# GpSimd issues the gathers of two units in a row, then the scatters of two units, and a scatter waits for the third one ahead of it instead of for the whole unit ahead

## The chip, the cores and the metric

The kernel runs on one core of a Trainium2 chip. A core has five engines that run their own instruction streams: TensorE (PE in the profile, with PEld for its weight loads), VectorE (DVE), ScalarE (ACT), GpSimd (POOL) and SyncE (SP). They meet at semaphores. The metric is the device time of one execution in microseconds; shorter is better.

## The reference

There are 50,000 nodes with 128 features and 50,000 edges, sorted by receiver. Each edge takes its sender's features, projects them, mixes them with its direction and with weights from a small network of its length, and adds the result to its receiver. Each node is then normalised.

```python
xs = s @ W_up0 / f32(MUL) ** 0.5
xv = jnp.einsum('nmc,mk->nkc', v, W_up1) / f32(MUL) ** 0.5
ss = xs[senders]                       # gather
vv = xv[senders]
m0 = w[:, 0] * ss                      # w: the network's weights of the edge
m1 = w[:, 1][:, :, None] * ss[:, :, None] * Y1[:, None, :]
m2 = w[:, 2][:, :, None] * vv
m3 = w[:, 3] * (jnp.einsum('emc,ec->em', vv, Y1) / SQ3)
msg_s = jax.ops.segment_sum(mid_s, receivers, num_segments=num_nodes)   # scatter and add
msg_v = jax.ops.segment_sum(mid_v, receivers, num_segments=num_nodes)
x = _layernorm(x + out, axis=-1)       # out: the projected sums
```

The input draws the receivers as 50,000 times the square of a uniform number and sorts them, so that nodes of low number have many edges and nodes of high number have few.

## The kernel before

The edges are cut into 98 units (UNITS) of four tiles (G); a tile is 128 edges. They are worked off from the high receivers down. For each tile GpSimd issues a gather (`sender<-in_x_dram,index`, L420), an indirect DMA that fetches 128 rows of x by the edges' senders. TensorE transposes and projects the rows, computes the weights and sums edges of one tile that have the same receiver; VectorE makes the products; ScalarE moves results out of PSUM and writes the unit's message (`msg`, L641 and L642) into one of four slots (RING). Then GpSimd issues for each tile a scatter (`acc<-msg,index`, L444), an indirect DMA that adds 128 rows of the message onto the array acc in HBM. acc starts as a copy of x, made in 80 pieces that SyncE issues (L295) while the first units run. Once no later unit can touch a chunk of nodes, SyncE loads it from acc (L331), VectorE takes its moments, ScalarE normalises it, and SyncE stores it (L345); a table (`dense_orders`) says after which pair of units each chunk may be loaded.

Two scatters that add to the same row must not be in flight together. Within a tile this is met by the sums; between tiles by waits. A scatter counts up a semaphore of its own when it lands. In the kernel before, the first scatter of a unit waits for all four of the unit ahead (L435). The others wait for the one just ahead of them only if the table `scatter_orders` flags that two tiles of the unit have overlapping ranges of receivers (`meets`), except in units 0 and 1, where they always wait (L442). So that neighbouring tiles do not stand in one unit, `turns` (L272) deals the eight tiles of two rows of edges out to an even and an odd unit.

The order on GpSimd is written out by hand (L448 to L456): the gathers of six units (LAG), then for each unit v the four gathers of unit v + 6 and the four scatters of unit v. A gather waits, at the first tile of a unit, for all gathers of two units ahead (L416) and for TensorE to have used the slot of eight units ahead (L418). The message slots tie ScalarE to GpSimd: the message of unit v waits until the scatters of unit v - 4 have landed (L640).

## Time and profile before

| | us |
|---|---|
| median of three runs | 1323.9 (1321.33 to 1324.72) |
| the profiled execution | 1335.3 |
| its span, first to last instruction | 1333.5 |
| granted TensorE clock, mean | 0.831 |
| GpSimd busy | 1014.3 (76% of the span) |
| TensorE busy | 928.8 (70%) |
| VectorE busy | 692.2 (52%) |
| ScalarE busy | 537.5 (40%) |

An indirect DMA is issued by GpSimd; its busy time in the profile is the time in which it makes the descriptors, and the data land afterwards. Between two such instructions the profile shows about 0.30 us in which the engine is idle and waits for nothing that the profile shows ("issue"). "remote" is a wait whose releaser the profile cannot name.

### The profile page before, as it was taken

The numbers are of one execution on the slowest core, as the hardware profiler recorded it, in microseconds if no ns is written. First come the engines' busy times: TensorE is split into PE (matmuls) and PEld (weight loads), VectorE is DVE, ScalarE is ACT, GpSimd is POOL, SyncE is SP. The second block draws the span as 40 slices with busy tenths as digits, with TensorE's granted clock in tenths as the row PEclk, the third lists the DMA queues.
The fourth block names the chain that finished last, engine by engine and source line by source line (L and its number), as shares of the span: only waits on it lengthen the run. The fifth ranks groups of instructions, "written<-read, shape, count | busy, mean of one in ns | idle before, by whom it ended". The sixth has DMA issues, their size and how long they took to land.

```text
span 1333.5 us, 25760 instructions
## 1 busy us (share of the span) xinstructions
PE 928.8 (70%) x6206; PEld 871.6 (65%) x6206; DVE 692.2 (52%) x2882; ACT 537.5 (40%) x1403; POOL 1014.3 (76%) x817
## 2 busy tenths in 40 slices
PE   2577688787788867776876768777876766767800
PEld 1477577787677766766776767676776766767700
DVE  5364334465576456556556466465465556555402
ACT  5233233244445534444444444434443434534301
POOL 6347878888888888888888888888888888888761
PEclk7588877887888889889879897788788888898955
DMA  4377786433443443453453453443444444443332
GB/s 131 113 184 161 168 185 120 94 65 67 114 97 67 93 116 69 90 119 69 90 120 67 91 118 69 93 110 73 94 92 91 94 92 93 93 91 68 59 28 63
DMA packets 82548, 130.36 MB, mean 98 GB/s; under 512 B 16168, under 2 KB 66763, under 8 KB 81232
## 3 DMA queue, kind: packets, MB, share of 16 engines
q0 software_dynamic: 68992, 51.43, 28.7%
q1 hardware_dynamic: 12888, 77.27, 17.3%
q10 hardware_dynamic: 632, 1.29, 0.3%
q14 instruction: 27, 0.22, 0.1%
q8 instruction: 9, 0.15, 0.0%
HBM read 78.31 MB, written 77.22 MB: 117 GB/s over the span
## 4 chain that ended last, share of the span: by engine, by line
issue 31%; POOL 28%; DMA 11%; PE 8%; another core or an unknown queue 7%; SPq 5%; ACT 4%; POOLq 3%; ACTq 1%; DVE 0%; DVEq 0%
POOL acc L444 20%; POOL sender L420 7%; DMA acc<-msg,index 6%; DMA acc<-in_x_dram 5%; SPq L295 3%; PE ps_msg L553 2%; PE ps_sum L541 2%; ACT normed L693 2%; PE ps_wts L528 2%; POOLq L427 1%; PE ps_hid L512 1%; PE ps_dst L494 1%; PE ps_sT L500 1%; ACT hid L656 1%
## 5 line engine op out<-in xcount | busy, mean ns | idle before, releaser
L444 POOL DMA_INDIRECT acc<-msg,index x392 | 621.1, 1585 | 170.3 <-issue 111.0
L420 POOL DMA_INDIRECT sender<-in_x_dram,index x392 | 386.8, 987 | 123.5 <-issue 111.9
L541 PE MATMUL ps_sum<-same,mid 128*128 128x128 f32 x1568 | 248.0, 310 | 1.5 <-issue 0.8
L541 PEld LDWEIGHTS ps_sum<-same,mid 128*128 128x128 f32 x1568 | 240.3, 226 | 10.0 <-DVE mid L930 0.8
L915 DVE TENSOR_TENSOR wts<-ps_wts,bias 128x512 f32<-128x512 f32 x98 | 67.8, 692 | 323.2 <-PE ps_wts L528 205.4
L528 PE MATMUL ps_wts<-mlp,hid 128*128 128x128 f32 x784 | 139.4, 335 | 104.9 <-ACT hid L668 100.6
L632 ACT COPY sumT<-ps_sum 128x512 f32<-128x512 f32 x196 | 114.9, 587 | 235.5 <-remote 131.3
L553 PE MATMUL ps_msg<-outw,sumT 128*128 128x64 f32 x1568 | 202.0, 285 | 2.3 <-ACT sumT L632 1.6
L553 PEld LDWEIGHTS ps_msg<-outw,sumT 128*128 128x128 f32 x1568 | 200.0, 206 | 3.2 <-issue 1.2
L528 PEld LDWEIGHTS ps_wts<-mlp,hid 128*128 128x128 f32 x784 | 126.6, 245 | 111.8 <-ACT hid L668 107.0
L512 PE MATMUL ps_hid<-hid,mlp 128*128 128x256 f32 x196 | 78.8, 490 | 150.2 <-ACT hid L656 110.1
L693 ACT ACTIVATE normed<-total,shift,rstd 128x128 f32 x391 | 157.0, 484 | 56.4 <-DVE shift L981 50.4
L908 DVE TENSOR_TENSOR proj<-ps_up,vec_all 128x384 f32<-128x384 f32 x98 | 54.4, 555 | 208.0 <-remote 137.9
L521 PE MATMUL ps_up<-up,senderT 128*128 128x128 f32 x784 | 131.9, 319 | 28.8 <-issue 10.4
L512 PEld LDWEIGHTS ps_hid<-hid,mlp 128*128 128x128 f32 x196 | 35.8, 228 | 162.6 <-ACT hid L656 118.6
L641 ACT COPY msg<-ps_msg 128x128 f32 (+1 forms) x98 | 26.1, 266 | 283.6 <-DMA acc<-msg,index 134.8
L521 PEld LDWEIGHTS ps_up<-up,senderT 128*128 128x128 f32 x784 | 111.2, 219 | 43.1 <-issue 21.8
L944 DVE BATCH_NORM_STATS2 stats<-total 128x6 f32 x391 | 79.5, 278 | 56.8 <-DMA total<-acc 56.2
L881 DVE CUSTOM_DVE_ANT_0 junk<-same,earlier 128x128 f32<-128x128 f32 x392 | 91.4, 289 | 3.4
L507 PE MATMUL ps_hid<-basisT,mlp 32*128 32x128 f32 x392 | 75.4, 315 | 13.8 <-ACT basisT L648 9.8
L650 ACT COPY senderT<-ps_sT 128x512 f32<-128x512 f32 x98 | 56.8, 579 | 62.3 <-remote 32.3
L500 PE MATMUL ps_sT<-ident,sender 128*128 128x128 f32 x392 | 71.5, 314 | 8.9 <-DMA sender<-in_x_dram,index 8.9
(135 smaller groups left out, 1061.5 us busy)
## 6 DMA issues: line engine op xcount, KB each, us to landing
acc<-in_x_dram SPq DMA_DIRECT2D x80, 312.5 KB
total<-acc SPq DMA_DIRECT2D x30, 832.0 KB
out_dram<-normed SPq DMA_DIRECT2D x29, 832.0 KB
sender<-in_x_dram,index POOLq DMA_INDIRECT x392
acc<-msg,index POOLq DMA_INDIRECT x392
out_dram<-normed ACTq DMA_DIRECT2D x1, 832.0 KB
vec_raw<-in_edge_attr_dram SPq DMA_DIRECT2D x1, 576.0 KB
acc<-zeros SPq DMA_DIRECT2D x1, 320.0 KB, 3.9
```

The costliest lines, as they stand in the source:

```text
L420: pool.indirect_dma_start(sender[:, u % SRING, i, :], None, x, bass.IndirectOffsetOnAxis(ap=index[:, u, 0, i:i + 1], axis=0)).then_inc(gat ...
L444: pool.indirect_dma_start(acc, bass.IndirectOffsetOnAxis(ap=index[:, v, 1, i:i + 1], axis=0), msg[:, v % RING, i, :], None, compute_op=ALU.add
L500: mm = pe.transpose(ps_sT[:, P * i:P * (i + 1)], sender[:, k % SRING, i, :], ident[:, :])
L512: pe.matmul(ps_hid[:, 2:4, :], mlp1[:, :], hid0[:, k % 2, :], start=True, stop=True).then_inc(hid1_ps, 1)
L521: mm = pe.matmul(ps_up[:, i, :], senderT[:, b, P * i:P * (i + 1)], up[:, :], start=True, stop=True)
L528: mm = pe.matmul(ps_wts[:, i, :], hid1[:, b, P * (i // 2):P * (i // 2 + 1)], mlp2[:, i % 2, :], start=True, stop=True)
L541: mm = pe.matmul(ps_sum[r][:, i, h, :], mid[:, b, 2 * r + i, P * h:P * (h + 1)], same[:, b, 2 * r + i, :], start=True, stop=True)
L553: mm = pe.matmul(ps_msg[:, i, 2 * MUL * h:2 * MUL * (h + 1)], sumT[:, b, i, h, :], outw[:, h, :], start=True, stop=True)
L632: act.copy(sumT[:, b, 2 * r:2 * r + 2, :, :], ps_sum[r][:, :, :, :]).then_inc(sum_ready[r], 1)
L693: mm = act.activation(normed[0:parts, b, r, :], total[0:parts, quarter, r, :].rearrange("p b d -> p (b d)"), ACT.Identity, scale=rstd[0:pa ...
L881: mm = dve.tensor_tensor_reduce(junk[:, b, i, :], same[:, b, i, :], earlier[:, :], 1.0, 0.0, ALU.mult, ALU.add, count[:, b, i:i + 1])
L944: mm = dve.bn_stats(stats[0:parts, r, :], total[0:parts, quarter, r, :].rearrange("p b d -> p (b d)"))
```

## The change

LAG stays at six, and BATCH = 2 is new. After the first six units' gathers, GpSimd issues the gathers of units v + 6 and v + 7 in a row, eight of them, and then the eight scatters of units v and v + 1.

Count all scatters through, n = 4v + i. Scatter n now waits for scatter n - 3 to have landed, always. It waits for n - 1 (and, at the first tile of a unit, for n - 2) only if the unit's flag is set; without the flag that wait asks for a count that an older landing has already brought. The flag is now made from the ranges of tiles one and two places apart in this count, over unit borders too. `turns` deals the tiles in another order within the unit, so that those at distance one and two are not neighbours. The extra waits for units 0 and 1 are gone.

Each gather now has its own semaphore by tile (`gathered`, and `slot_done` for the first two units), and gather i of unit u waits for gather i of unit u - 1, four issues ahead. `slot_done` is the new name of `scattered` and starts with the 16 counts of a gather, so all that is compared with it is 16 higher. TensorE waits for the four gathers of its unit one by one. The table of flags takes other instructions on VectorE, and one more memset on GpSimd.

```diff
 LAG = 6
+BATCH = 2
...
-        meet = sb("meet", [1, UNITS, G * (G - 1) // 2])
-        meet_too = sb("meet_too", [1, UNITS, G * (G - 1) // 2])
+        meet = sb("meet", [1, 2, TILES])
+        meet_too = sb("meet_too", [1, 2, TILES])
...
-            return a.rearrange("p (j w) (q r) -> p w q j r", w=2, r=2)[:, w]
+            return a.rearrange("p (j w) (r q) -> p w q j r", w=2, r=2)[:, w]
...
-                    sp.wait_ge(scattered[1][i], 16 * j + 16)
+                    sp.wait_ge(slot_done[1][i], 16 * j + 32)
...
+            pool.memset(meet[:, :, :], 0.0)
...
+            def landed(n):
+
+                return slot_done[n // G % 2][n % G], 16 * (n // G // 2) + 32
+
+            def here(u, i):
+
+                return (slot_done[u][i], 16) if u < 2 else (gathered[u % 2][i], 16 * (u // 2))
+
             def gathers(u):
 
-                if u >= 2:
-                    pool.wait_ge(gathered[u % 2], 16 * G * (u // 2))
                 if u >= SRING:
                     pool.wait_ge(senderT_ps, u - SRING + 1)
                 for i in range(G):
+                    if u >= 1:
+                        pool.wait_ge(*here(u - 1, i))
                     pool.indirect_dma_start(sender[:, u % SRING, i, :], None, x,
                                             bass.IndirectOffsetOnAxis(ap=index[:, u, 0, i:i + 1], axis=0)
-                                            ).then_inc(gathered[u % 2], 16)
+                                            ).then_inc(here(u, i)[0], 16)
...
-                if v >= 1:
-                    for i in range(G):
-                        pool.wait_ge(scattered[1 - c][i], 16 * ((v + 1) // 2))
                 for i in range(G):
-                    if i >= 1:
-
-                        if v >= 2:
-                            pool.wait_ge(scattered[c][i - 1], 16 * (v // 2) + 16 * meets)
-                        else:
-                            pool.wait_ge(scattered[c][i - 1], 16)
+                    n = G * v + i
+                    if n >= 3:
+                        pool.wait_ge(*landed(n - 3))
+                    for of in (n - 2, n - 1) if i == 0 else (n - 1,):
+                        if of >= 0:
+
+                            to, count_after = landed(of)
+                            pool.wait_ge(to, count_after - 16 + 16 * meets)
...
-            for v in range(UNITS):
-                if v + LAG < UNITS:
-                    gathers(v + LAG)
-                scatters(v)
+            for v in range(0, UNITS, BATCH):
+                for u in range(v + LAG, min(v + LAG + BATCH, UNITS)):
+                    gathers(u)
+                for u in range(v, v + BATCH):
+                    scatters(u)
...
-                pe.wait_ge(gathered[b], u * (16 * G // 2) + 16 * G - 16 * G * b // 2)
...
+                    if k < 2:
+                        pe.wait_ge(slot_done[b][i], 16)
+                    else:
+                        pe.wait_ge(gathered[b][i], 8 * (u - b))
                     mm = pe.transpose(ps_sT[:, P * i:P * (i + 1)], sender[:, k % SRING, i, :], ident[:, :])
...
-                        act.wait_ge(scattered[b][i], 8 * (v - b) - 8 * RING + 16)
+                        act.wait_ge(slot_done[b][i], 8 * (v - b) - 8 * RING + 32)
...
-                at = 0
-                for apart in range(1, G):
-                    n = G - apart
-                    dve.tensor_tensor(meet[:, :, at:at + n], high[:, :, 0:n], low[:, :, apart:G], ALU.is_ge)
-                    mm = dve.tensor_tensor(meet_too[:, :, at:at + n], high[:, :, apart:G], low[:, :, 0:n], ALU.is_ge)
-                    at += n
+                lo, hi = (a[:, :, :].rearrange("p v i -> p (v i)") for a in (low, high))
+                for apart in range(1, 3):
+                    n = TILES - apart
+                    dve.tensor_tensor(meet[:, apart - 1, apart:TILES], hi[:, 0:n], lo[:, apart:TILES], ALU.is_ge)
+                    mm = dve.tensor_tensor(meet_too[:, apart - 1, apart:TILES], hi[:, apart:TILES], lo[:, 0:n], ALU.is_ge)
                 link(mm)
...
```

**Order on GpSimd at the start.** The engine's stream from the last gathers before the first scatter on, before; `sender` is the gathers' target, `acc<-msg` a scatter, and the names in brackets are the semaphores that a row waits for.

```order
L420 DMA sender<-in_x_dram,index 128x128 [waits gathered0,scatter_tables,spare_rows]
L420 DMA sender<-in_x_dram,index 128x128 x3
L427 TENSOR_LOAD scatter_orders
L427 ISA x2
L428 ISA
L429 ISA [waits acc_init0]
L444 DMA acc<-msg,index 50640x128 [waits msg_ready,acc_init1,rows_ready]
L444 DMA acc<-msg,index 50640x128 [waits scattered0_0]
L444 DMA acc<-msg,index 50640x128 [waits scattered0_1]
L444 DMA acc<-msg,index 50640x128 [waits scattered0_2]
```

And now:

```order
L431 DMA sender<-in_x_dram,index 128x128 [waits gathered0_0]
L431 DMA sender<-in_x_dram,index 128x128 [waits gathered0_1]
L431 DMA sender<-in_x_dram,index 128x128 [waits gathered0_2]
L431 DMA sender<-in_x_dram,index 128x128 [waits gathered0_3]
L437 TENSOR_LOAD scatter_orders
L437 ISA x2
L438 ISA
L439 ISA [waits acc_init0]
L453 DMA acc<-msg,index 50640x128 [waits msg_ready,acc_init1,rows_ready]
L451 ISA
L453 DMA acc<-msg,index 50640x128 [waits slot_done0_0]
L453 DMA acc<-msg,index 50640x128 [waits slot_done0_1]
```

Before, the gathers of unit 6 are the last ahead of the first scatter, and each further scatter of unit 0 waits for the one ahead. Now the gathers of unit 7 stand ahead of the first scatter too, and the waits for the scatter just ahead ask only for a count that the gather of the slot brought; the fourth scatter waits for the first.

**Order on GpSimd in the middle.** The stream from unit 8's gathers to unit 9's, before:

```order
L420 DMA sender<-in_x_dram,index 128x128 [waits senderT_ps,gathered0]
L420 DMA sender<-in_x_dram,index 128x128 x3
L427 TENSOR_LOAD scatter_orders
L427 ISA x2
L428 ISA
L429 ISA [waits acc_init0]
L444 DMA acc<-msg,index 50640x128 [waits scattered1_1,scattered1_2,scattered1_0,scattered1_3,msg_ready,acc_init1,rows_ready]
L440 ISA
L444 DMA acc<-msg,index 50640x128 [waits scattered0_0]
L444 DMA acc<-msg,index 50640x128 [waits scattered0_1]
L444 DMA acc<-msg,index 50640x128 [waits scattered0_2]
L420 DMA sender<-in_x_dram,index 128x128 [waits senderT_ps,gathered1]
```

And now, from unit 3's scatters to the gathers that follow:

```order
L439 ISA [waits acc_init0]
L451 ISA [waits msg_ready,slot_done0_1,rows_ready,acc_init1]
L453 DMA acc<-msg,index 50640x128 [waits slot_done0_2,slot_done0_3]
L453 DMA acc<-msg,index 50640x128 [waits slot_done0_2,slot_done1_0]
L453 DMA acc<-msg,index 50640x128 [waits slot_done0_3,slot_done1_1]
L453 DMA acc<-msg,index 50640x128 [waits slot_done1_0,slot_done1_2]
L431 DMA sender<-in_x_dram,index 128x128 [waits gathered1_0,senderT_ps]
L431 DMA sender<-in_x_dram,index 128x128 [waits gathered1_1]
L431 DMA sender<-in_x_dram,index 128x128 [waits gathered1_2]
L431 DMA sender<-in_x_dram,index 128x128 [waits gathered1_3]
L431 DMA sender<-in_x_dram,index 128x128 [waits gathered0_0,senderT_ps]
L431 DMA sender<-in_x_dram,index 128x128 [waits gathered0_1]
```

Before, four gathers and four scatters take turns, and the first scatter waits for four landings at once. Now eight of a kind stand in a row; each scatter names two semaphores, one of the third scatter ahead, and each gather names one.

**Order on GpSimd at the end.** The last two units, where no gathers are left, before:

```order
L440 ISA
L444 DMA acc<-msg,index 50640x128 [waits scattered0_0]
L444 DMA acc<-msg,index 50640x128 [waits scattered0_1]
L444 DMA acc<-msg,index 50640x128 [waits scattered0_2]
L427 TENSOR_LOAD scatter_orders
L427 ISA x2
L428 ISA
L429 ISA [waits acc_init0]
L444 DMA acc<-msg,index 50640x128 [waits scattered0_1,scattered0_2,scattered0_0,scattered0_3,msg_ready,acc_init1,rows_ready]
L440 ISA
```

And now:

```order
L453 DMA acc<-msg,index 50640x128 [waits slot_done1_2,slot_done1_3]
L451 REGISTER_ALU [waits slot_done1_2]
L453 DMA acc<-msg,index 50640x128 [waits slot_done0_0]
L453 DMA acc<-msg,index 50640x128 [waits slot_done1_3,slot_done0_1]
L453 DMA acc<-msg,index 50640x128 [waits slot_done0_0,slot_done0_2]
L437 TENSOR_LOAD scatter_orders
L437 ISA x2
L438 ISA
L439 ISA [waits acc_init0]
L451 ISA [waits msg_ready,slot_done0_1,rows_ready,acc_init1]
L453 DMA acc<-msg,index 50640x128 [waits slot_done0_2,slot_done0_3]
L453 DMA acc<-msg,index 50640x128 [waits slot_done0_2,slot_done1_0]
```

The wait for the whole unit ahead has gone from the unit's first scatter; what stands there now names tiles 1, 2 and 3 of the unit ahead, of which only tile 1 must have landed when the flag is not set.

## Rows read from the trace of the kernel before

**Rows 1.** Page, busy us, share of the span and instructions.
```profile
PE 928.8 (70%) x6206; PEld 871.6 (65%) x6206; DVE 692.2 (52%) x2882; ACT 537.5 (40%) x1403; POOL 1014.3 (76%) x817
```

**Rows 2.** Groups of POOL by line: busy, mean ns; idle before, releasers.
```profile
L444 POOL DMA_INDIRECT acc<-msg,index x392 | 621.1, 1585 | 170.3 <-issue 111.0 <-DMA acc<-msg,index 37.9 <-ACT msg L642 20.5
L420 POOL DMA_INDIRECT sender<-in_x_dram,index x392 | 386.8, 987 | 123.5 <-issue 111.9 <-DMA acc<-msg,index 6.4 <-DVE index L753 4.3
```

**Rows 3.** Waits of POOL's scatters for landings: us in total, times, longest.
```profile
POOL acc L444 <- DMA acc<-msg,index: 37.9, 24, 3.8
```

**Rows 4.** Timeline of POOL, start: start us, us, what, idle before.
```profile
46.88 0.95 POOL L420 DMA_INDIRECT sender<-in_x_dram,index  x1 [0.30 <-issue]
68.34 1.64 POOL L444 DMA_INDIRECT acc<-msg,index  x1 [20.51 <-ACT msg L642]
73.10 1.57 POOL L444 DMA_INDIRECT acc<-msg,index  x1 [3.13 <-DMA acc<-msg,index]
```

**Rows 5.** Timeline of POOL, middle: gathers of a unit, scatters of a unit.
```profile
704.83 1.02 POOL L420 DMA_INDIRECT sender<-in_x_dram,index  x1 [0.30 <-issue]
706.15 0.98 POOL L420 DMA_INDIRECT sender<-in_x_dram,index  x1 [0.30 <-issue]
707.44 0.95 POOL L420 DMA_INDIRECT sender<-in_x_dram,index  x1 [0.30 <-DMA acc<-msg,index]
...
709.94 1.62 POOL L444 DMA_INDIRECT acc<-msg,index  x1 [0.30 <-issue]
711.87 1.58 POOL L444 DMA_INDIRECT acc<-msg,index  x1 [0.30 <-issue]
...
715.62 1.60 POOL L444 DMA_INDIRECT acc<-msg,index  x1 [0.30 <-issue]
```

**Rows 6.** Timeline of POOL, the end: unit 91's last scatter, unit 92's first, the last.
```profile
1249.24 1.57 POOL L444 DMA_INDIRECT acc<-msg,index  x1 [0.30 <-issue]
1253.37 1.55 POOL L444 DMA_INDIRECT acc<-msg,index  x1 [2.56 <-DMA acc<-msg,index]
...
1307.45 1.57 POOL L444 DMA_INDIRECT acc<-msg,index  x1 [0.30 <-issue]
```

**Rows 7.** Timeline of SP after the last scatter.
```profile
1312.17 0.35 SPq L331 DMA_DIRECT2D total<-acc  x1
```

**Rows 8.** Timeline of ACT: the messages of units 0, 1, 2 and 9.
```profile
66.69 0.69 ACT L642 COPY msg<-ps_msg 128x384 f32<-128x384 f32 x1
...
74.24 0.67 ACT L642 COPY msg<-ps_msg 128x384 f32<-128x384 f32 x1
...
92.11 0.69 ACT L642 COPY msg<-ps_msg 128x384 f32<-128x384 f32 x1
...
182.18 0.69 ACT L642 COPY msg<-ps_msg 128x384 f32 x1
```

**Rows 9.** Timeline of POOL: the first scatter of unit 9.
```profile
199.87 1.62 POOL L444 DMA_INDIRECT acc<-msg,index  x1 [0.30 <-issue]
```

**Rows 10.** Timeline of PE and DVE during the first gathers.
```profile
34.50 2.07 PE L521 MATMUL ps_up<-up,senderT 128*128 128x128 f32 x8
...
52.26 0.56 DVE L908 TENSOR_TENSOR proj<-ps_up,vec_all 128x384 f32<-128x384 f32 x1 [17.40 <-remote]
```

**Rows 11.** Timeline of ACT: the messages of units 52 and 53.
```profile
707.71 0.67 ACT L642 COPY msg<-ps_msg 128x384 f32 x1
719.33 0.68 ACT L642 COPY msg<-ps_msg 128x384 f32 x1
```

**Rows 12.** Timeline of POOL: the last scatter of unit 48.
```profile
702.92 1.60 POOL L444 DMA_INDIRECT acc<-msg,index  x1 [0.30 <-issue]
```

**Rows 13.** Page, DMA issues: the transfers of the chunks.
```profile
total<-acc SPq DMA_DIRECT2D x30, 832.0 KB
out_dram<-normed SPq DMA_DIRECT2D x29, 832.0 KB
```

**Rows 14.** Timeline of DVE: the first instruction after the flags' table.
```profile
28.75 0.36 DVE L785 TENSOR_SCALAR norm<-norm 128x392 f32<-128x392 f32 x1 [3.37 <-ACT norm L609]
```

More of the change, by code:

```diff
@@ L61 @@
 RSQRT_BITS = float(0x5f3759df)
-assert UNITS % 2 == 0 and LAG <= SRING and (UNITS - 2) % SRING == 0 and UNITS <= P and FULL == UNITS - 1 and FULL >= 96
+assert UNITS % 2 == 0 and LAG <= SRING and UNITS % BATCH == 0 and LAG % BATCH == 0 and (UNITS - 2) % SRING == 0 and UNITS <= P and FULL == UNITS - 1 and FULL >= 96
 assert NORM_AFTER > STATS_AFTER and NORM_AFTER > RING // 2 and (UNITS - 2) % RING == 0 and CHUNKS % 2 == 0 and PIECES % 2 == 0 and N % PIECE == 0 and REST <= P
@@ L208, in bass_gnn @@
         sp_passed = sem("sp_passed")
-        gathered = [sem(f"gathered{b}") for b in range(2)]
+        gathered = [[sem(f"gathered{b}_{i}") for i in range(G)] for b in range(2)]
         basis_staged = sem("basis_staged")
@@ L234, in bass_gnn @@
         msg_ready = sem("msg_ready")
-        scattered = [[sem(f"scattered{b}_{i}") for i in range(G)] for b in range(2)]
+        slot_done = [[sem(f"slot_done{b}_{i}") for i in range(G)] for b in range(2)]
         total_in = [sem(f"total_in{b}") for b in range(2)]
@@ L419, in gathers @@
                 for i in range(G):
+                    if u >= 1:
+                        pool.wait_ge(*here(u - 1, i))
                     pool.indirect_dma_start(sender[:, u % SRING, i, :], None, x,
                                             bass.IndirectOffsetOnAxis(ap=index[:, u, 0, i:i + 1], axis=0)
-                                            ).then_inc(gathered[u % 2], 16)
+                                            ).then_inc(here(u, i)[0], 16)
             def scatters(v):
-                c = v % 2
                 order = pool.value_load(scatter_orders[0:1, v:v + 1], min_val=2, max_val=2 * PIECES - 1)
@@ L445, in scatters @@
                                             msg[:, v % RING, i, :], None, compute_op=ALU.add
-                                            ).then_inc(scattered[c][i], 16)
+                                            ).then_inc(slot_done[v % 2][i], 16)
             pool.wait_ge(index_in, 1)
@@ L801, in make_scatter_orders @@
             def make_scatter_orders():
-                at = 0
-                for apart in range(1, G):
-                    n = G - apart
-                    dve.tensor_tensor(meet[:, :, at:at + n], high[:, :, 0:n], low[:, :, apart:G], ALU.is_ge)
-                    mm = dve.tensor_tensor(meet_too[:, :, at:at + n], high[:, :, apart:G], low[:, :, 0:n], ALU.is_ge)
-                    at += n
-                link(mm)
-                link(dve.tensor_tensor(meet[:, :, :], meet[:, :, :], meet_too[:, :, :], ALU.mult))
-                link(dve.tensor_reduce(meet_unit[:, :], meet[:, :, :], AX_X, ALU.max))
+                lo, hi = (a[:, :, :].rearrange("p v i -> p (v i)") for a in (low, high))
[3 more added lines that the diff above has]
+                    mm = dve.tensor_tensor(meet_too[:, apart - 1, apart:TILES], hi[:, apart:TILES], lo[:, 0:n], ALU.is_ge)
+                link(mm)
+                for apart in range(1, 3):
+                    mm = dve.tensor_tensor(meet[:, apart - 1, apart:TILES], meet[:, apart - 1, apart:TILES],
+                                           meet_too[:, apart - 1, apart:TILES], ALU.mult)
+                link(mm)
+                link(dve.tensor_tensor(meet[:, 0, :], meet[:, 0, :], meet[:, 1, :], ALU.max))
+                link(dve.tensor_reduce(meet_unit[:, :], meet[:, 0, :].rearrange("p (v i) -> p v i", i=G), AX_X, ALU.max))
                 link(dve.tensor_reduce(pieces[:, :], high[:, :, :], AX_X, ALU.max))
```

## The prediction

> **What bounds the kernel now.** I read the shares of the engines first. None is near 100%: GpSimd is busy for 76% of the span, TensorE for 70% [rows 1]. The groups by line say what that hides. GpSimd issues 784 indirect DMAs, busy 621.1 + 386.8 = 1007.9 us, and ahead of each stands the 0.30 us that the profile calls issue, 784 x 0.30 = 235 us [rows 2]. Together that is 1243 us of a span of 1333.5 us. The timeline of the middle shows the same: gathers and scatters follow each other at 0.30 us, and GpSimd waits for nobody [rows 5]. So GpSimd's issue is the path, and a change is worth what it takes out of GpSimd's stream or out of its waits. What is left of the span are the first 11.6 us, a wait of 20.51 us for the first message [rows 4], waits for landings, and the end after the last scatter (1307.45 + 1.57 to 1333.5, 24.5 us), which loads, normalises and stores the last chunk [rows 6, 7].
>
> The waits view gives the third of these. Scatters wait for landings 24 times, 37.9 us in all, 3.8 us at the longest [rows 3]. Less the 0.30 us of issue that each has anyway, 24 x 0.30 = 7.2 us, 30.7 us are true waits. The timeline says where: three within unit 0 and three within unit 1, the first of them 3.13 us [rows 4], and one ahead of each of units 92 to 97, where no gathers are left to issue in the meantime. The first of those six is 2.56 us, 2.26 us over issue [rows 6]; six of them make 13.6 us, and 17.1 us remain for units 0 and 1. The other twelve of the 24 end within the issue time. In units 2 to 91 a unit's first scatter comes 5 us of gathers after the last scatter of the unit ahead, and the wait is over by then.
>
> **The change part by part.** The sum is made against the profiled execution (span 1333.5 us, 1335.3 us with what lies around it) and taken off the median, 1323.9 us. The profiled one is 11.4 us longer; I don't know where, and that matters below.
>
> *The end.* Units 92 to 97 no longer wait for the last scatter, but for the third one ahead. From the end of its issue to the due time of the scatter in question lie two further scatters and three times issue, about 2 x 1.57 + 3 x 0.30 = 4.04 us [rows 6]. The wait for the nearest landing lasted 2.56 us, so the new wait is over in time. Saved: 13.6 us. What is late next here is nothing of TensorE's: the message slots are full (below), and a unit of scatters takes 7.5 us.
>
> *The start.* Units 0 and 1 lose their six waits (17.1 us). Also, the gathers of unit 7 now come ahead of the first scatter, into the 20.51 us in which GpSimd waits for message 0: four gathers at 0.95 + 0.30 and 0.10 for the switch (next but one), 5.1 us that are not on the path any more. That would be 22.2 us. But GpSimd would then run into the messages. They are ready at 67.38, 74.91 and 92.80 us for units 0 to 2, and at 182.87 us for unit 9 [rows 8], whose scatter starts at 199.87 us [rows 9]: 17.0 us of slack, the least that I found among units 3 to 17. From message 0 to its scatter it took 68.34 - 67.38 = 0.96 us [rows 4, 8]. So not more than 17.0 - 0.96 = 16.0 us can be had unless the messages come faster, and I take 16.0 us. Units 0 to 3 themselves fit: scatters of units 0 and 1 to 68.34 + 8 x 1.87 = 83.3 us, eight gathers to 93.4 us, and message 2 is there at 92.8 us. One bound is the full 22.2 us. The other: VectorE started on unit 0 at 52.26 us, though TensorE had its input ready at 36.57 us, and what released it the profile can't name [rows 10]; that is 4.4 us after the last gather's end at 47.83 us [rows 4]. If the early gathers are what holds the other engines back, the four more of unit 7 move every message by 5.1 us, and 10.9 us are left.
>
> *Fewer switches.* The first two gathers after scatters take 1.02 and 0.98 us against 0.95, the first two scatters after gathers 1.62 and 1.58 us [rows 5] against 1.55 and 1.57 where none came between [rows 6]. A pair of units has one switch each way less: 0.10 us from the gathers, up to 0.08 us from the scatters if none of it is the load of the table, which stays. 46 pairs with gathers: 4.6 to 8.3 us. I take 6.
>
> *New waits, scatters.* Scatters 3 to 7 of a run of eight wait for one that was issued in the same run, with the same 4.04 us of room. The landings that the rows show are seen 2.56 us after the end of the issue at the end of the program and at most 3.8 us in units 0 and 1, beside the copies of x. In the middle, ScalarE writes a message as soon as the scatters of four units ahead have landed: unit 53's starts 1.95 us after the issue's end (719.33 - 0.16 for the copy ahead of it, less 715.62 + 1.60), unit 52's 3.03 us (707.55 less 702.92 + 1.60) [rows 5, 11, 12]. All within the room, so the lower end is nothing lost. The upper end: 59 chunks are loaded or stored meanwhile [rows 13]. If each pushed one landing past the longest seen by half of its spread over the shortest, (3.8 - 2.56) / 2 = 0.62 us, 3.8 + 0.62 - 4.04 = 0.38 us would be lost 59 times, 22 us. The nearest rows, those of the middle, are at the lower end; I take 8 us, for gathers and scatters together.
>
> *New waits, gathers.* Each waits for the fourth one ahead; the room is three gathers at 1.25 and 0.30, 4.05 us, as wide as for scatters. Behind a gather that waits stand the rest of the run and then the scatters, so a loss here is as dear. It is in the 8 us.
>
> *More semaphores per instruction.* The first scatter of a unit, with seven semaphores and a table load, has the same 0.30 us ahead of it as the others and is 0.07 us longer [rows 5]. 0.01 us for each of 780 instructions with one more wait would be 7.8 us; I take nothing, since the sequencer does it while the instruction ahead runs.
>
> *Others.* The flags' table is rebuilt on VectorE with longer rows; VectorE then idles 3.37 us for ScalarE [rows 14], which hides the half microsecond. The other order of tiles within a unit costs nothing. TensorE's clock plays no part: message 52 is written between the scatters of units 48 and 49 [rows 5, 11, 12], over three units early, and that slack of some 40 us hides that the message slots now come free in pairs.
>
> Sum: 16.0 + 13.6 + 6 - 8 = 27.6 us, 1323.9 - 27.6 = 1296 us.
>
> **The rivals.** (a) The messages don't limit the start. Half of the 11.4 us by which the profiled execution is longer may be just the unnamed waits of the other engines; without them messages come sooner and the start gives 22.2 us. With the losses as above 34 us are saved (1290 us), with none and the full 8.3 us of switches 44 us (1280 us). Against it: the slack of 17.0 us is a row.
>
> (b) The early gathers hold back the messages: 10.9 at the start, 22.5 us in all, 1301 us; with the upper 22 us for lost room 8.5 us, 1315 us. For it speaks the 4.4 us between the last gather and VectorE's start.
>
> (c) Slower than before: with eight scatters in a row the landing of each takes longer, because three of them are in flight with no gathers between. In a run of eight, scatter 3 waits for 0 and scatter 6 for 3, so a landing seen x us beyond the room costs 2x in each of 49 pairs. The gain without losses is 35.6 us; it is gone at 35.6 / 98 = 0.36 us, that is from landings at 4.40 us on. At 3.8 + 1.24 (the whole spread once more) = 5.04 us the cost is 98 x 1.00 = 98 us, and the kernel takes 1323.9 + 62 = 1386 us. Against it: scatters in a row at the end land in 2.56 us.
>
> The rows show a landing 1.95 to 3.8 us after the issue. The Trainium skill, "DMA: Bandwidth & Descriptors", section "Latency and other measured facts", says that HBM answers in 0.2 us on average and in 2 us at high load, and that this is most of a DMA's fixed cost. By that rule a loaded stretch would add 1.8 us to the 2.56 us, 4.36 us, 0.32 us over the room, 31 us in 98 waits, and leave 4 us of gain (1320 us). The spread from 1.95 to 3.8 us agrees that load matters; that it reaches this far everywhere no row shows.
>
> (d) The change doesn't do what it says: the flag is set for most units, so each scatter waits for the one ahead as in unit 0. That is 2.26 us for each of some 380 scatters, 860 us. In the kernel before no unit but 0 and 1 waits within the unit, so no two tiles at that distance overlap, and the new order keeps tiles at distance one and two equally far apart.
>
> **How the numbers follow.** Forecast 0.50; (a) 0.24; (b) 0.19; (c), the case of the skill's rule included, 0.06; (d) 0.01. The forecast's own range is 1290 to 1302 us. Taking in most of (a) and of (b), I reach from 1282 to 1311 us. A measurement can tell 0.3% from no change, 4 us. All of the forecast, (a) and nearly all of (b) are faster than that: 0.92. No change needs (b) with more losses than its upper end, or the skill's rule: 0.04. Slower is the rest of (c) and (d): 0.04.
>
> **What would show it.** In the profile after: the gathers of unit 7 ahead of the first scatter; no wait within unit 0, and a wait for messages in the first 200 us; after the last gather 24 scatters and more in a row at 1.87 us, without a gap of 2.56 us; pairs of units at about 25.2 us instead of 25.4; POOL's waits for landings below 10 us in all, each well under 1 us. Wrong would be: waits for landings at scatters 3 and 6 of most runs, waits for messages after the first 250 us, or a first message later than 70 us.

## The result, and the profile after

The changed kernel takes 1285.41 us (median of four runs, 1283.88 to 1289.08); the kernel before took 1323.8 us beside it (four runs, 1321.33 to 1324.72). The ratio is 0.9717, with a 95% interval of 0.9692 to 0.9742: 37.5 us faster by the ratio, where 27.6 us were forecast. The time lies in the predicted range of 1282 to 1311 us, 10.6 us under the predicted value.

The profiled execution of the changed kernel took 1289.08 us, with a span of 1287.3 us. From its page, the engines' busy time (us, share of the span, instructions) and POOL's two groups by line (busy, mean ns; idle time ahead, releaser), to be read against [rows 1, 2]:

```profile
PE 862.5 (67%) x6206; PEld 819.2 (64%) x6206; DVE 693.7 (54%) x2882; ACT 535.3 (42%) x1403; POOL 1005.5 (78%) x818
...
L453 POOL DMA_INDIRECT acc<-msg,index x392 | 617.3, 1575 | 128.6 <-issue 110.2
L431 POOL DMA_INDIRECT sender<-in_x_dram,index x392 | 381.0, 972 | 127.8 <-issue 110.4
```

GpSimd is busy for 8.8 us less. The greater part went from its idle time: 170.3 to 128.6 us ahead of the scatters, while the gathers gave back 4.3 us. The wait for a message, 20.5 us in the row of before, has gone from the list.

The waits of POOL (us in total, times, longest), against [rows 3]:

```profile
POOL acc L453 <- issue: 110.2, 344, 1.3
POOL acc L453 <- DMA acc<-msg,index: 14.2, 40, 1.0
POOL sender L431 <- DMA sender<-in_x_dram,index: 12.2, 25, 2.5
```

Each of them contains the 0.30 us of issue. Over all 784 instructions, what goes beyond issue (0.31 us at the most) comes to 9.0 us ahead of the scatters and 4.9 us ahead of the gathers, if GpSimd's wait for its first indices is left out; part of it stands under "issue" (1.3 us at the longest), where the profile names no releaser. Some 11 of these 13.9 us fall ahead of unit 20, where copies of x still run beside.

The start on POOL's timeline (start us, us, what, idle before), against [rows 4]:

```profile
52.87 1.03 POOL L431 DMA_INDIRECT sender<-in_x_dram,index  x1 [0.30 <-DMA acc<-in_x_dram]
54.21 1.63 POOL L453 DMA_INDIRECT acc<-msg,index  x1 [0.30 <-DMA acc<-in_x_dram]
56.15 1.57 POOL L453 DMA_INDIRECT acc<-msg,index  x1 [0.30 <-issue]
58.02 1.55 POOL L453 DMA_INDIRECT acc<-msg,index  x1 [0.30 <-issue]
...
62.56 1.55 POOL L453 DMA_INDIRECT acc<-msg,index  x1 [0.94 <-DMA acc<-in_x_dram]
...
80.51 1.62 POOL L453 DMA_INDIRECT acc<-msg,index  x1 [0.30 <-issue]
...
86.86 1.56 POOL L453 DMA_INDIRECT acc<-msg,index  x1 [0.91 <-DMA acc<-msg,index]
...
157.57 0.94 POOL L431 DMA_INDIRECT sender<-in_x_dram,index  x1 [2.49 <-DMA sender<-in_x_dram,index]
```

The first scatter follows the last gather of unit 7 at once, 14.1 us earlier than in [rows 4], and the next two come at issue distance. The message is not what it waits for: ACT's timeline has messages 0, 1 and 2 far ahead of their place in [rows 8].

```profile
52.42 0.69 ACT L655 COPY msg<-ps_msg 128x384 f32<-128x384 f32 x1
...
59.97 0.67 ACT L655 COPY msg<-ps_msg 128x384 f32<-128x384 f32 x1
...
75.61 0.69 ACT L655 COPY msg<-ps_msg 128x384 f32<-128x384 f32 x1
```

Message 0 is ready at 53.11 us against 67.38 us, and message 1 at 60.64 us, ahead of unit 1's first scatter at 62.56 us. Nothing in the change makes messages come 14 us sooner. This was the first thing to settle.

The middle, a run of eight scatters and the gathers after it, against [rows 5]:

```profile
695.99 1.62 POOL L453 DMA_INDIRECT acc<-msg,index  x1 [0.30 <-issue]
697.92 1.59 POOL L453 DMA_INDIRECT acc<-msg,index  x1 [0.30 <-issue]
...
711.00 1.02 POOL L431 DMA_INDIRECT sender<-in_x_dram,index  x1 [0.30 <-issue]
712.33 0.98 POOL L431 DMA_INDIRECT sender<-in_x_dram,index  x1 [0.30 <-issue]
...
721.29 1.62 POOL L453 DMA_INDIRECT acc<-msg,index  x1 [0.31 <-issue]
```

The pair takes 721.29 - 695.99 = 25.30 us, and nothing in it waits. The slower first two of a kind come once in a pair.

The end, where a gap of 2.56 us stood ahead of units 92 to 97 [rows 6]: the last scatter of unit 91, the first two of unit 92, the last of all.

```profile
1216.22 1.57 POOL L453 DMA_INDIRECT acc<-msg,index  x1 [0.30 <-issue]
1218.09 1.55 POOL L453 DMA_INDIRECT acc<-msg,index  x1 [0.30 <-issue]
1219.95 1.66 POOL L453 DMA_INDIRECT acc<-msg,index  x1 [0.30 <-DMA acc<-msg,index]
...
1261.15 1.57 POOL L453 DMA_INDIRECT acc<-msg,index  x1 [0.30 <-issue]
```

### The profile page after: what moved, and what is told of

It reads as the page before. It is cut to its first block, busy times and chain, and to the rows that moved or that the text cites. A ratio compares the mean times of both kernels' runs of the same rounds, so it can differ in the third digit from the quotient of the medians.

```text
span 1287.3 us, 25626 instructions
## 1 busy us (share of the span) xinstructions
PE 862.5 (67%) x6206; PEld 819.2 (64%) x6206; DVE 693.7 (54%) x2882; ACT 535.3 (42%) x1403; POOL 1005.5 (78%) x818
## 3 DMA queue, kind: packets, MB, share of 16 engines
q1 hardware_dynamic: 12888, 77.27, 17.1%
## 4 chain that ended last, share of the span: by engine, by line
POOL 38%; DMA 27%; issue 24%; DVE 3%; POOLq 3%; PE 2%; SPq 2%; ACT 1%; DVEq 0%; ACTq 0%
POOL acc L453 22%; POOL sender L431 15%; DMA acc<-msg,index 13%; DMA acc<-in_x_dram 12%; DMA sender<-in_x_dram,index 3%; POOLq L437 1%; DVE stats L960 1%; PE ps_sum L554 1%; SPq L297 1%; PE ps_wts L541 1%; PE ps_hid L525 0%; POOLq L452 0%; POOLq L451 0%; DMA total<-acc 0%; ACT normed L706 0%
## 5 line engine op out<-in xcount | busy, mean ns | idle before, releaser
L453 POOL DMA_INDIRECT acc<-msg,index x392 | 617.3, 1575 | 128.6 <-issue 110.2
L431 POOL DMA_INDIRECT sender<-in_x_dram,index x392 | 381.0, 972 | 127.8 <-issue 110.4
L525 PE MATMUL ps_hid<-hid,mlp 128*128 128x256 f32 x196 | 86.3, 532 | 334.7 <-ACT hid L669 334.7
L566 PE MATMUL ps_msg<-outw,sumT 128*128 128x64 f32 x1568 | 186.0, 272 | 0.0
L566 PEld LDWEIGHTS ps_msg<-outw,sumT 128*128 128x128 f32 x1568 | 182.8, 192 | 0.0
L541 PE MATMUL ps_wts<-mlp,hid 128*128 128x128 f32 x784 | 133.1, 326 | 0.6 <-ACT hid L681 0.6
L534 PE MATMUL ps_up<-up,senderT 128*128 128x128 f32 x784 | 116.2, 292 | 5.8 <-DVE mid L938 5.8
L534 PEld LDWEIGHTS ps_up<-up,senderT 128*128 128x128 f32 x784 | 97.3, 195 | 17.8 <-issue 6.4
L924 DVE TENSOR_TENSOR proj<-ps_up,vec_all 128x384 f32<-128x384 f32 x98 | 54.1, 552 | 73.2 <-issue 39.5
L520 PE MATMUL ps_hid<-basisT,mlp 32*128 32x128 f32 x392 | 70.3, 299 | 0.3 <-ACT basisT L661 0.2
L504 PE MATMUL ps_dst<-ident,dst_now 128*128 128x128 f32 x392 | 67.2, 300 | 0.0
```

Of the source, the lines that this page charges most:

```text
L431: pool.indirect_dma_start(sender[:, u % SRING, i, :], None, x, bass.IndirectOffsetOnAxis(ap=index[:, u, 0, i:i + 1], axis=0)).then_inc(her ...
L453: pool.indirect_dma_start(acc, bass.IndirectOffsetOnAxis(ap=index[:, v, 1, i:i + 1], axis=0), msg[:, v % RING, i, :], None, compute_op=ALU.add
L520: mm = pe.matmul(ps_hid[:, q, :], mlp0[:, q, :], basisT[:, b, :], start=True, stop=True)
L525: pe.matmul(ps_hid[:, 2:4, :], mlp1[:, :], hid0[:, k % 2, :], start=True, stop=True).then_inc(hid1_ps, 1)
L534: mm = pe.matmul(ps_up[:, i, :], senderT[:, b, P * i:P * (i + 1)], up[:, :], start=True, stop=True)
L541: mm = pe.matmul(ps_wts[:, i, :], hid1[:, b, P * (i // 2):P * (i // 2 + 1)], mlp2[:, i % 2, :], start=True, stop=True)
```

## The experiments

The runs fall in two groups, each on one chip with the kernel before timed beside it: 1324.52 us (median of 17) for the first four, 1324.47 us (of 9) for the other four. The changed kernel's 1285.4 us comes from its own four runs, so a step of a few microseconds against it is given by the ratios too. Lengths of GpSimd's stretches are taken from the timeline of each profiled execution: up to the first scatter of unit 0, of 4, of 20 and of 90, to the end of the last scatter, and to the end of the span.

| execution | to unit 0 | 0 to 3 | 4 to 19 | 20 to 89 | 90 to 97 | end | span |
|---|---|---|---|---|---|---|---|
| before, first | 68.3 | 67.9 | 204.3 | 890.4 | 78.1 | 24.5 | 1333.5 |
| before, again | 51.9 | 72.7 | 202.9 | 891.1 | 78.8 | 24.4 | 1321.7 |
| after, first | 54.2 | 52.8 | 210.1 | 885.8 | 59.9 | 24.6 | 1287.3 |
| after, again | 54.1 | 52.1 | 206.5 | 887.4 | 59.6 | 24.4 | 1284.1 |
| scatters' waits only | 49.6 | 51.4 | 204.9 | 894.8 | 64.7 | 24.4 | 1289.9 |
| two in a row, old waits | 53.2 | 81.4 | 224.8 | 968.1 | 76.1 | 24.4 | 1428.1 |
| one unit at a time | 49.8 | 51.7 | 204.7 | 892.5 | 64.9 | 24.4 | 1287.9 |
| old gathers' waits | 54.5 | 52.1 | 204.7 | 882.6 | 59.6 | 24.5 | 1277.8 |
| fourth ahead | 55.7 | 50.5 | 202.0 | 882.9 | 59.7 | 24.6 | 1275.3 |

### The kernel before, profiled once more

No edit. It asks whether the 20.51 us of [rows 4] belong to the kernel or to that one execution.

> The kernel before, profiled once more. In its first profile the other engines stood still during the first gathers (VectorE starts on unit 0 at 52.26 us, the first scatter at 68.34 us); in the profile after they did not (first scatter at 54.21 us). Theory A, it belongs to the kernel (up to eight gathers in flight instead of four): first scatter within 2 us of 68.3 again, span 1330 to 1337. Rival N, it is a matter of the one execution: first scatter anywhere from 54 to 68 us, the span shorter by as much.

It took 1323.51 us, like the median, with a span of 1321.7 us. Its timeline of POOL, the last gather of unit 6 and unit 0's scatters:

```profile
47.77 0.95 POOL L420 DMA_INDIRECT sender<-in_x_dram,index  x1 [0.30 <-issue]
51.93 1.64 POOL L444 DMA_INDIRECT acc<-msg,index  x1 [3.21 <-DMA acc<-in_x_dram]
57.84 1.57 POOL L444 DMA_INDIRECT acc<-msg,index  x1 [4.27 <-DMA acc<-msg,index]
63.48 1.67 POOL L444 DMA_INDIRECT acc<-msg,index  x1 [4.07 <-DMA acc<-msg,index]
69.17 1.55 POOL L444 DMA_INDIRECT acc<-msg,index  x1 [4.02 <-DMA acc<-msg,index]
```

The first scatter starts at 51.93 us, not at 68.34 us. The profile names a copy of x as what released it; message 0 is done at 50.28 + 0.69 = 50.97 us, and the 0.96 us from there to the scatter are those of [rows 4, 8], so it may have waited for both. The idle time is 3.21 us in any case, not 20.51. The waits within the unit are longer instead, 4.0 to 4.3 us against the 3.13 us of [rows 4]. The copies of x may be why, though no run parts them from the rest: they are issued until 184 us here and until 218 us in the other execution. Beyond issue, GpSimd waits 24.0 us up to the end of unit 3, 2.9 of them ahead of the first scatter, and 13.9 us at the end. Its waits (us in total, times, longest), which answer to [rows 3] too:

```profile
POOL acc L444 <- DMA acc<-msg,index: 41.6, 21, 4.3
...
POOL acc L444 <- DMA acc<-in_x_dram: 3.8, 3, 3.2
```

So the 20.51 us and the late messages were that execution's alone. This execution is the one to hold the changed kernel against.

### Only the gathers' new waits, in the kernel before

```diff
-                if u >= 2:
-                    pool.wait_ge(gathered[u % 2], 16 * G * (u // 2))
...
+                    m = G * u + i - 4
+                    if m >= 0:
+                        pool.wait_ge(gathered[m // G % 2][m % G], 16 * (m // G // 2) + 16)
```

> The kernel before with only the gathers' waits of the change: gather i of a unit waits for gather i of the unit ahead. Theory A: first scatter near 54 us in the profile instead of 68, time 1307 to 1314 us (14 us from the start, less up to 5 us for waits of gathers). Rival N: within 3 us of the kernel before or up to 5 us slower, 1321 to 1329 us.

1326.01 us, ratio 1.0006, interval 0.9991 to 1.0022: no difference. The theory that gave this part the start's 14 us fell; the first scatter stands at 50.8 us in its profile, close to the 51.9 us of the second execution of before. With four scatters between two units' gathers, the fourth gather ahead has always landed.

### Only the scatters' waits

The changed kernel with BATCH = 1 and the old wait of the gathers: the waits three ahead, the flags' table and the order of the tiles are new, the order of units is the old one.

```diff
-BATCH = 2
+BATCH = 1
...
+                if u >= 2:
+                    for i in range(G):
+                        pool.wait_ge(*here(u - 2, i))
...
-                    if u >= 1:
-                        pool.wait_ge(*here(u - 1, i))
```

> The change without the gathers' waits (first tile of a unit waits for all of two units ahead, as before) and without the two units in a row (one by one, as before); only the scatters' waits, the table and the order of tiles are new. The sum says 17.1 + 13.4 us of waits gone, less some 9 us of new ones: 1302 us under both theories (1298 to 1306). If the messages limit the start, as the prediction had it, one more us is lost. Profile under A: first scatter near 68 us; under N anywhere from 54.

1291.68 us, ratio 0.9752 (0.9728 to 0.9776), 32.8 us faster than before: 10 us better than expected, and by itself nearly the whole gain. The sum behind the expectation took 30.5 us of waits off and put 9 us of new ones on; in the profiles all waits beyond issue are 37.9 us in the second of before and 2.3 us here. What the other order of the tiles does by itself was not run.

### Only two units in a row, with the old waits

```diff
-            for v in range(UNITS):
-                if v + LAG < UNITS:
-                    gathers(v + LAG)
-                scatters(v)
+            for v in range(0, UNITS, BATCH):
+                for u in range(v + LAG, min(v + LAG + BATCH, UNITS)):
+                    gathers(u)
+                for u in range(v, v + BATCH):
+                    scatters(u)
```

> The kernel before with only the order of the change: gathers of two units, then scatters of two units, all waits as before. Each second unit's first scatter then waits for the whole unit just ahead with nothing issued in between: 2.26 us in 46 pairs more, 104 us; the order itself gives 5.1 + up to 8.8 us. Expected 1410 to 1420 us. If the landing of a scatter in such a run takes longer than at the program's end, more: rival (c) of the prediction would show more than 3.5 us at each of these waits.

1425.74 us, ratio 1.0757 (1.0731 to 1.0782), 101 us slower. The waits and a piece of the timeline, the border between two units of a pair:

```profile
POOL acc L445 <- DMA acc<-msg,index: 148.4, 56, 6.3
```

```profile
725.01 1.56 POOL L445 DMA_INDIRECT acc<-msg,index  x1 [0.30 <-issue]
729.11 1.55 POOL L445 DMA_INDIRECT acc<-msg,index  x1 [2.53 <-DMA acc<-msg,index]
```

Each pair now has inside it the wait that the kernel before had only at its end: 2.53 - 0.30 = 2.23 us in each of 46 pairs are 103 us. The time is 5.7 us over the range expected, which ended at 1420 us. From unit 20 on, the waits for landings at such borders last 2.5 to 2.8 us, so the case that the expectation named for rival (c), over 3.5 us at each, isn't seen; beside the copies of x, ahead of unit 20, they reach 6.3 us. So two units in a row are worth something only with the scatters' new waits, and the two parts' times don't add: -32.8 and +101 against -37.5 us together.

### The changed kernel, profiled once more

No edit.

> The changed kernel, profiled once more. In its first profile the waits over 0.30 us of scatters come to 9.0 us and those of gathers to 4.9 us, most of them before unit 20. If these belong to the kernel, both come back within 3 us, and the span is 1282 to 1288 us; if they are chance, they do not.

1285.86 us, span 1284.1 us, the first scatter at 54.06 us as before. Waits beyond issue are 6.6 us ahead of scatters and 3.7 us ahead of gathers, 10.3 us in all, against 13.9 us in the first profile, so these waits belong to the kernel. Here the gathers' lead:

```profile
POOL sender L431 <- DMA sender<-in_x_dram,index: 14.6, 36, 1.5
POOL acc L453 <- DMA acc<-msg,index: 10.9, 28, 1.5
```

### The changed kernel with the gathers' old wait

The same exchange of the gathers' waits as above; BATCH stays 2.

> The changed kernel with the gathers' waits of before: a unit's first gather waits for all four gathers of two units ahead, the others for nothing. Theory: the 4.9 us of waits of gathers over issue in the profile of the changed kernel are on the path and go, the scatters' waits stay; 1280 us (1278 to 1283). Rival: as the gathers' waits alone made no difference to the kernel before, they make none here, 1283 to 1288 us, because what a gather does not wait the next scatter waits.

1279.80 us, ratio 0.9662 (0.9636 to 0.9688), as the theory said. The gathers' excess waits are gone, the scatters' are 4.5 us, and the time is 5.6 us under the 1285.4 us of the changed kernel (7.3 us by the ratios). Against the second profile of the changed kernel all excess waits fell by 5.8 us and the span by 6.3 us. So what a gather waits is on the path.

### The changed kernel with one unit at a time

```diff
-BATCH = 2
+BATCH = 1
```

> The changed kernel with one unit at a time (BATCH = 1): waits of scatters and gathers as in the change. The scatters' waits alone, one unit at a time, gave 1291.7 us. Theory: gathers' waits cost nothing one unit at a time, since the fourth gather ahead is then behind four scatters, so 1290 to 1294 us, and the two units in a row are worth some 6 us net: 8.8 us less busy time, less the new waits. Rival: the two in a row are worth nothing, the time is that of the changed kernel, 1284 to 1287 us.

1291.54 us, ratio 0.9747 (0.9721 to 0.9773). Two in a row are worth 6.1 us with the gathers' new waits (1291.5 to 1285.4) and 11.9 us with the old ones (1291.7 to 1279.8). The first of these is 4.0 us by the ratios, whose intervals overlap a little, though no run of one kernel lies among those of the other. Its two groups of POOL show from where:

```profile
L453 POOL DMA_INDIRECT acc<-msg,index x392 | 627.8, 1602 | 122.3 <-issue 118.3
L431 POOL DMA_INDIRECT sender<-in_x_dram,index x392 | 382.6, 976 | 122.8 <-issue 102.7
```

Busy time is 10.5 us longer for the scatters and 1.6 us for the gathers than in the changed kernel's first profile, and idle time 6.3 and 5.0 us shorter.

### A wait for the fourth scatter ahead

The step that the runs point to: gathers wait as in the kernel before, and scatters for the fourth one ahead, with flags for distances one to three; tiles are dealt so that those up to three apart are not neighbours.

```diff
-                    if n >= 3:
-                        pool.wait_ge(*landed(n - 3))
-                    for of in (n - 2, n - 1) if i == 0 else (n - 1,):
+                    if n >= 4:
+                        pool.wait_ge(*landed(n - 4))
+                    for of in (n - 3, n - 2, n - 1) if i == 0 else (n - 1,):
```

> The changed kernel with the gathers' waits of before and a scatter that waits for the fourth one ahead instead of the third, the flags made for distances one to three, and the tiles of a unit dealt out in falling order so that none at these distances are neighbours. Room for a landing is then 4.04 + 1.87 = 5.91 us, over all landings seen. Theory: the 9.0 us of scatters' waits go as well as the 4.9 us of gathers', 1272 us (1269 to 1277). Rival: landings take longer with four in flight, or GpSimd then runs into the messages or the copies of x early on: less than 5 us under the changed kernel, 1280 to 1285 us.

1277.08 us (1276.22 to 1277.36), ratio 0.9633 (0.9608 to 0.9659), 5 us over the value expected and just past the upper edge of its range (1277 us), but faster than both kernels. No wait lasts longer than issue:

```profile
POOL acc L455 <- DMA acc<-msg,index: 9.8, 32, 0.3
POOL sender L433 <- DMA acc<-msg,index: 5.2, 17, 0.3
```

The scatters' 4.5 us were to be had, and 2.7 us came out; GpSimd was busy for 1007.6 us, 2.3 us more than with the wait three ahead.

## Why the prediction was right, and where not

What bounds the kernel was read rightly: GpSimd's stream. The second execution of before and the second of after differ by 37.6 us, and the stretches of the table add up to it: +2.1 up to the first scatter, -20.5, +3.7, -3.7, -19.2, and nothing at the end. So do the engine's own sums: 8.8 us less busy (1015.1 to 1006.3 us) and 28.7 us less idle ahead of its 784 DMAs (281.3 to 252.6 us).

In the terms of the prediction that is 23.5 us for the start and 14.1 us for the end, the moved gathers counted with the start; in units 4 to 89 fewer switches and new waits cancel. The sum had 16.0, 13.6 and -2. It was too low by 10 us, three quarters of them from the start, and the forecast's own range, 1290 to 1302 us, was missed; the measured time lies in the wider range because that one took in most of rival (a).

*The end*, 13.6 us: right. The waits that go were 13.9 us; the stretch is shorter by 19.2 us, of which 5.1 are the gathers of one unit that have moved to the front. That scatters in a row land within the room of 4.04 us is shown by the row at 1218.09.

*The start*, 16.0 us: this is the step that failed, by its cap. "So not more than 17.0 - 0.96 = 16.0 us can be had unless the messages come faster": they did come faster. The slack of 17.0 us, the 20.51 us and the late messages [rows 4, 8, 9, 10] were all read from one execution in which the other engines stood still early. In the second one message 9 is done at 147.89 + 0.67 = 148.56 us and its scatter starts at 187.94 us, a slack of 39.4 us instead of 17.0. In the changed kernel the messages of units 0 to 3 are ready 1.1, 1.9, 4.2 and 4.9 us ahead of their first scatters in the first profile (5.3 to 8.8 us in the second), and that of unit 9 by 41.0 us. So messages are close behind only in the first four units, and never late. The start gave 20.5 - 2.1 + 5.1 = 23.5 us, close to the 22.2 us that stood there without the cap, though by other amounts: more from waits (21.1 us behind the first scatter in units 0 to 3 instead of 17.1, against some 1 us that is left there), less from the moved gathers. The prediction let them vanish in the idle stretch; that stretch is 3.21 us, and the first scatter comes 2.1 us later than before, so they are worth 3.0 us.

*Fewer switches*, 6 us out of 4.6 to 8.3: the size was right, and something came on top that no row had shown. GpSimd's busy time fell by 8.8 us. Against the kernel that differs in nothing but BATCH it fell by 11.2 to 12.0 us in the two executions. Take the median of each of the sixteen places in a pair over units 20 to 89, with the second scatter at its usual 1.58 us: a pair is busy for 20.41 us with one unit at a time and for 20.24 us with two. That is 0.17 us a pair, 8 us in 46 pairs. The rest is single long scatters. In four of the five profiles with one unit at a time the second scatter of every other unit often takes up to 1.97 us instead of 1.58, as here (the changed kernel with one unit at a time):

```profile
688.79 1.62 POOL L453 DMA_INDIRECT acc<-msg,index  x1 [0.30 <-issue]
690.71 1.86 POOL L453 DMA_INDIRECT acc<-msg,index  x1 [0.30 <-issue]
```

Of the 392 scatters, 3 and 16 take over 1.75 us in the two executions of before, 34 with only the gathers' waits, 30 with only the scatters' waits and 23 with one unit at a time, but 0 to 7 in the five executions with two units in a row. Why is open.

*More semaphores*, nothing: no sign of a cost. The kernel with only the scatters' waits has scatters busy for 630.4 us, against 621.1 and 625.9 us in two executions of before; but the kernel with only the gathers' waits, whose scatters wait as before, has 631.4 us. Most of what makes these differ is the long scatters.

*New waits*, 8 us out of 0 to 22: close, 10.3 and 13.9 us. The prediction feared the chunk transfers of the middle. They are one of two places; the other is ahead of unit 20, beside copies of x, with 11 of the 13.9 us and 5.6 of the 10.3 us. There a scatter that ended at 80.51 + 1.62 = 82.13 us is seen landed only at 86.86 us, 4.73 us later, and a gather that ended at 151.30 us only at 157.57 us, 6.27 us later. From unit 20 to unit 89 the two profiles have 12 and 16 waits beyond issue, 3.1 and 4.7 us in all, each under 0.6 us. Every one of the 28 is over 3.1 to 6.9 us after SyncE issued a chunk's load or store, the longest of them like this (SyncE and GpSimd in the second profile):

```profile
939.15 0.36 SPq L347 DMA_DIRECT2D out_dram<-normed  x1
```

```profile
944.29 0.94 POOL L431 DMA_INDIRECT sender<-in_x_dram,index  x1 [0.89 <-DMA sender<-in_x_dram,index]
```

So the mechanism of the upper end, a landing pushed past the room by a chunk, does occur, as far as its timing tells; but 51 chunk transfers fall in that stretch, and they cost under 0.1 us each instead of 0.38. Over the whole middle the last packet of a scatter has passed 1.4 us after the end of its issue (median), and away from the chunks the room is ample. That a loss ahead of a gather is as dear as one ahead of a scatter was right, as the run with the gathers' old wait shows.

*The rivals.* (a) was the mechanism: messages don't limit the start, and the second profile bears out its guess that the unnamed waits were part of the 11.4 us. Its 1290 us, and the 1280 us without losses, lie on both sides of 1285.4. (b) is out: in five profiles with unit 7's gathers ahead message 0 is ready at 48.4 to 53.1 us, in four without them (the first of before apart) at 48.7 to 51.0 us; what moves it is told at the end. (c) occurred as a mechanism but seldom: landings beyond 4.40 us exist beside copies of x and, seldom, behind a chunk's transfer, and the waits are 13.9 us in all, not 98 of them. For the rule of the Trainium skill on HBM's answer under load ("DMA: Bandwidth & Descriptors", "Latency and other measured facts"), the runs speak both ways: landings of 4.73 us beside the copies, and of up to 4.62 us behind a chunk's transfer in the middle, are at least as late as the 4.36 us estimated from it, but nearly all landings of the middle, where 45% of the DMA engines' time is in use on average, fit in the room. At what load its 2 us would hold, no run here shows. (d) is out: the scatters of the middle don't wait.

Of the signs named: unit 7's gathers ahead of the first scatter, 24 scatters in a row at 1.87 us, no gap of 2.56 us and 25.3 us for a pair (25.2 foretold, 25.5 in the second profile of before) came. A wait for messages in the first 200 us did not, which is the failed cap again. The waits were to be under 10 us and each well under 1 us; they were 13.9 and 10.3 us, and one reached 2.5.

## What to carry to other kernels

An idle stretch near the start that a profile can't name a releaser for, in an execution that is itself longer than the median, is worth a second profile before it becomes a cap or a term. Where one engine's issue is the path, ask of each wait how far back it reaches: in this kernel a wait for the landing just ahead costs it in full (2.2 us) at every place where nothing else is left to issue, one for the third ahead is nearly free, and at one for the fourth GpSimd never waits. And two halves of such a change need not add: the order alone cost 101 us, the waits alone gained 33, both together gained 37.

## What the runs showed of the hardware that was not expected

One of ten profiled executions had a slow beginning on the engines other than GpSimd. The queue of SP's copies of x, in the window from 19 to 52 us, in the first profile of before, the second, and the changed kernel's:

```profile
21.33 30.11 SPq L295 DMA_DIRECT2D acc<-in_x_dram  x5
```

```profile
19.47 32.64 SPq L295 DMA_DIRECT2D acc<-in_x_dram  x16
```

```profile
19.46 32.10 SPq L297 DMA_DIRECT2D acc<-in_x_dram  x16
```

Five copies were issued in one case and sixteen in the two others (fifteen or sixteen in the remaining seven profiles). In the same execution VectorE's first product of unit 0, which [rows 10] has at 52.26 us after 17.40 us "remote", stands at 37.14 us in the second:

```profile
37.14 0.56 DVE L908 TENSOR_TENSOR proj<-ps_up,vec_all 128x384 f32<-128x384 f32 x1 [1.59 <-PE ps_up L521]
```

Waits for a "remote" releaser, 138 us on this line alone, occur in none of the other nine. GpSimd's gathers ran at their usual 0.95 us meanwhile. What held the other engines is not known and was not tried; the timed runs of before spread by some 10 us (1319.66 to 1329.39), so it may happen in a small way more often; no profile shows that.

The other surprise is how message 0 moves between profiles of one kernel: it is ready at 48.8 us in the changed kernel's second profile and at 53.1 us in its first. The same eight matmuls of units 0, 1 and 2 on PE, in the second and in the first:

```profile
34.37 2.08 PE L534 MATMUL ps_up<-up,senderT 128*128 128x128 f32 x8
...
40.93 1.13 PE L534 MATMUL ps_up<-up,senderT 128*128 128x128 f32 x8 [0.24 <-DVE mid L938]
...
48.45 1.16 PE L534 MATMUL ps_up<-up,senderT 128*128 128x128 f32 x8
```

```profile
35.06 2.08 PE L534 MATMUL ps_up<-up,senderT 128*128 128x128 f32 x8
...
43.63 2.08 PE L534 MATMUL ps_up<-up,senderT 128*128 128x128 f32 x8
...
52.79 1.16 PE L534 MATMUL ps_up<-up,senderT 128*128 128x128 f32 x8
```

Unit 0's run at 1.2 GHz in both, 3 us after an idle stretch of TensorE of some 17 us, and unit 1's at 2.4 GHz in one and still at 1.2 in the other. What lets the clock rise earlier in one of them was not tried. The granted clock by windows of the second profile (PE, PEld, DVE, ACT, POOL busy; then the clock, the DMA share and GB/s) agrees: 0.50 of full speed, then 1.00.

```profile
30.00:35.00 5.00, 3.79 (x16) 3.26 (x17) 4.90 (x11) 3.14 (x13) 3.78 (x5) 0.50 0.69 203
...
40.00:45.00 5.00, 4.76 (x39) 4.54 (x39) 4.16 (x18) 2.72 (x7) 3.78 (x5) 1.00 0.71 202
```

The first profile gives 1.00 for the same windows although its matmuls take twice as long, and its trace has no record of the clock ahead of 47 us at all, so the 1.00 says nothing there. The levels given above for it are read from the matmuls' durations. The first scatter starts at 54.2 and 54.1 us in the two all the same, since with eight gathers ahead it is no longer the message that it waits for.
